# The last ten GpSimd weight-sum pieces moved from ahead of the expert groups into the first five down groups

## The reference

```
xn  = layernorm(x)
s   = attention(xn)      # q, k, v projections; phi = elu + 1;
                         # running sum over the sequence of phi(k) * v, times phi(q) * scale; then Wo
f   = ffn(xn)            # router to 8 experts, top 2, capacity 256 tokens each;
                         # every expert uses the same w1 (4096 x 1024, exact gelu) and w2 (1024 x 4096)
out = x + s * silu(f)
```

## Time and profile before

| what | value |
|---|---|
| median of 3 runs | 2046.07 us (2045.12 to 2046.35) |
| the profiled execution, its time | 2045.16 us |
| its span in the trace | 2043.1 us |
| mean granted TensorE clock | 0.991 |
| PE busy | 1983.1 us, 97% |
| DVE busy | 1378.4 us, 67% |
| ACT busy | 695.9 us, 34% |
| POOL busy | 513.2 us, 25% |

### The profile page before, as it was taken

How to read it: one execution, slowest core, us unless ns; L and a number is a source line. 1 busy time by engine, 2 the same in 40 slices (tenths; PEclk the granted TensorE clock), 3 DMA queues, 4 the chain that set the end, 5 groups by cost and what they waited for, 6 DMA issues and landing times.

```text
span 2043.1 us, 27171 instructions
## 1 busy us (share of the span) xinstructions
PE 1983.1 (97%) x9396; PEld 905.2 (44%) x9396; DVE 1378.4 (67%) x2090; ACT 695.9 (34%) x1094; POOL 513.2 (25%) x640
## 2 busy tenths in 40 slices
PE   8979999999899999999999999999999999999996
PEld 2335444554434444444444444444444444444442
DVE  3778888878867767767777787474554555456656
ACT  1422232222553453444345353343222212213322
POOL 0098888888711101101100010030000000000002
PEclk9989999999999999999999999999999999999998
DMA  9576766667999777876767878783333333334635
GB/s 356 203 243 224 241 231 211 222 220 217 306 373 269 211 250 217 230 255 213 252 233 238 284 240 288 250 220 111 108 98 103 103 103 98 104 119 139 200 108 130
DMA packets 185259, 419.93 MB, mean 206 GB/s; under 512 B 18816, under 2 KB 73664, under 8 KB 182720
## 3 DMA queue, kind: packets, MB, share of 16 engines
q1 hardware_dynamic: 141776, 287.93, 42.3%
q0 software_dynamic: 34912, 121.71, 20.3%
q10 hardware_dynamic: 8464, 8.92, 1.4%
HBM read 268.51 MB, written 166.77 MB: 213 GB/s over the span
## 4 chain that ended last, share of the span: by engine, by line
PE 67%; POOL 15%; DMA 9%; DVE 4%; issue 3%; ACT 1%; SPq 0%; ACTq 0%; DVEq 0%; POOLq 0%
PE pair L2005 34%; PE pair L1976 31%; DMA arena<-w_down 3%; DMA arena<-w_up 3%; PE pair L1768 2%; POOL arena L723 2%; POOL arena L735 2%; POOL arena L737 1%; POOL arena L746 1%; POOL arena L739 1%; POOL arena L748 1%; POOL arena L750 1%; POOL arena L740 1%; POOL arena L751 1%; POOL up_sums L729 1%
## 5 line engine op out<-in xcount | busy, mean ns | idle before, releaser
L2005 PE MATMUL pair<-arena 128*128 128x512 f16 x3360 | 731.4, 379 | 9.6 <-DVE arena L1564 2.5
L1976 PE MATMUL pair<-xnT,arena 128*128 128x512 f16 x2400 | 528.5, 381 | 8.4 <-ACT xnT L962 4.1
L2005 PEld LDWEIGHTS pair<-arena 128*128 128x128 f16 x3360 | 326.9, 98 | 410.8 <-issue 17.6
L1818 PE MATMUL pair<-arena 128*128 128x512 f16 x1728 | 388.2, 383 | 8.4 <-DVE xnT L454 7.6
L1589 DVE SCALAR_TENSOR_TENSOR arena<-pair,arena 128x1024 f32<-128x1024 f32 x234 | 286.1, 1223 | 157.6 <-PE pair L2005 157.2
L1976 PEld LDWEIGHTS pair<-xnT,arena 128*128 128x128 f16 x2400 | 234.9, 98 | 295.4 <-ACT xnT L962 6.9
L1031 ACT ACTIVATE arena<-arena 128x512 f16<-128x512 f32 x280 | 170.0, 625 | 565.1 <-PE pair L2005 503.6
L1818 PEld LDWEIGHTS pair<-arena 128*128 128x128 f16 x1728 | 169.4, 98 | 205.4 <-issue 16.4
L1976 PE MATMUL pair<-xnT 128*128 128x512 f16 x960 | 213.8, 379 | 0.0
L1564 DVE SCALAR_TENSOR_TENSOR arena<-arena 128x512 f16<-128x512 f32 x280 | 189.1, 684 | 20.2 <-ACT arena L1031 18.3
L772 POOL DMA_DIRECT2D s_dram<-arena x8 | 6.2, 778 | 596.6 <-DVE arena L1589 581.4
(11 more groups left out here) (203 smaller groups left out, 1822.9 us busy)
## 6 DMA issues: line engine op xcount, KB each, us to landing
down_dram<-arena SPq DMA_DIRECT2D x70, 512.0 KB, 4.5
arena<-down_dram SPq DMA_DIRECT2D x70, 512.0 KB, 3.3
up_dram<-arena SPq DMA_DIRECT2D x100, 256.0 KB, 5.0
arena<-up_dram SPq DMA_DIRECT2D x100, 256.0 KB, 2.6
arena<-w_up POOLq DMA_DIRECT2D x40, 512.0 KB, 5.3
up_sums<-arena POOLq DMA_DIRECT2D x40, 512.0 KB, 3.6
arena<-w_down POOLq DMA_DIRECT2D x40, 512.0 KB, 5.2
down_sums<-arena POOLq DMA_DIRECT2D x40, 512.0 KB, 3.8
```

Source lines behind the costliest of these rows:

```text
L1818: ins = mm(out_bank(n), xT[u][:, a, c, :], wkv[:, (n // 2) * CH + c, b, e], start=(c == 0 and i == 0), stop=(c == CH - 1 and i == 2), skip ...
L1976: ins = mm(out_to, w[:, a, c * P:(c + 1) * P], x_in_op[:, b, c, :], start=(first and i == 0), stop=(i == 11), skip_group_check=True)
L2005: ins = mm(bank[2 + t // 2][:, (t % 2) * BLOCK:(t % 2 + 1) * BLOCK], g_ops[:, A_NAMES.index(DOWN_A[j]), c, a, t * P:(t + 1) * P], down_rin ...
```

## The change

The first 70 pieces are made as before. The last ten have a place of their own, `late_sums`: four rows of 256 f32 of `xnT` (the low part of x block "12", which no product reads once the sums of x are made, and where from group 7 on `kvq` lies). They are made one after another, two to a down, for downs 0 to 4: a load at point p = 0 (piece one) and p = 4 (piece two), the four operations and the store at p = 2 and p = 6. Each load waits for the store of the piece before; the first waits for the sums of x. ACT waits for 70 instead of 80 stores before it writes into `sum_ring`'s bytes, and for all 80 before its first load into `kvq`.

```
+        LATE_UNITS = 10
+        late_sums = xnT_rows[:, 8:12, HOLE:2 * HOLE]
...
+            def unit_at(u):
+                return late_sums if u >= len(UNITS) - LATE_UNITS else sum_ring[u % 3]
+
             def load_unit(u):
...
-                pool.dma_start(sum_ring[u % 3], src[:, :, c * (BLOCK // 2):(c + 1) * (BLOCK // 2)]).then_inc(sum_loaded[u % 3], 16)
+                pool.dma_start(unit_at(u), src[:, :, c * (BLOCK // 2):(c + 1) * (BLOCK // 2)]).then_inc(sum_loaded[u % 3], 16)
...
-            load_unit(0)
-            load_unit(1)
-            for u in range(len(UNITS)):
+            def make_unit(u):
                 if UNITS[u][0] == "up":
                     up_unit(u)
                 else:
                     down_unit(u)
                 store_unit(u)
-                if u + 2 < len(UNITS):
+
+            in_time = len(UNITS) - LATE_UNITS
+            load_unit(0)
+            load_unit(1)
+            for u in range(in_time):
+                make_unit(u)
+                if u + 2 < in_time:
                     if u >= 1:
                         pool.wait_ge(sum_stored[(u - 1) % 3], 16 * ((u - 1) // 3 + 1))
                     load_unit(u + 2)
...
                     pool.dma_start(out_rows[i, p], x_rows[i, p]).then_inc(copied, 16)
+
+                    u = in_time + 2 * i + p // 4
+                    if u < len(UNITS):
+                        if p % 4 == 0:
+                            if u == in_time:
+                                pool.wait_ge(xsum_done, 32)
+                            else:
+                                pool.wait_ge(sum_stored[(u - 1) % 3], 16 * ((u - 1) // 3 + 1))
+                            load_unit(u)
+                        elif p % 4 == 2:
+                            make_unit(u)
...
-                    stored(act, len(UNITS))
+                    stored(act, len(UNITS) - LATE_UNITS)
...
                         act.wait_ge(meta_ready, 1)
+                        stored(act, len(UNITS))
```

More of the change, by code:

```diff
@@ L728, in store_unit @@
                 pool.wait_ge(sum_made, 4 * u + 4)
-                pool.dma_start(to[:, :, c * (BLOCK // 2):(c + 1) * (BLOCK // 2)], sum_ring[u % 3]).then_inc(sum_stored[u % 3], 16)
+                pool.dma_start(to[:, :, c * (BLOCK // 2):(c + 1) * (BLOCK // 2)], unit_at(u)).then_inc(sum_stored[u % 3], 16)
             def up_unit(u):
-                w11, w12, w22, w21 = (sum_ring[u % 3][:, b, :] for b in range(4))
+                w11, w12, w22, w21 = (unit_at(u)[:, b, :] for b in range(4))
                 pool.wait_ge(sum_loaded[u % 3], 16 * (u // 3 + 1))
```

## The result

The changed kernel takes 2041.84 us (median of 8 runs, 2038.3 to 2043.41) against 2045.97 (8 runs) of the kernel before: ratio 0.9976, 95% interval 0.9967 to 0.9986, a gain of 4.9 us with 2.9 to 6.8 possible (the two medians are 4.1 us apart). The forecast was 2036.1 us, a gain of 10. The time lies just within the range given (2033 to 2042), the gain is a little under half of what was forecast.

The account below looks back on a forecast made before the run. PE was taken as busy for 1983.1 of 2043.1 us, with late loads causing waits before down 0. A gain of 10.5 us less 0.5 in the downs gave 10.0: 2036.1 us against 2046.07, range 2033 to 2042.

Parts of the forecast that it names:

- The chain's 15% for POOL: Chain of waits over the whole span: its 300 us for POOL can't be the pieces' cost, exceeding PE's 60 us idle.
- The signs: Before down 0: PE's waits fall from 9.8 to about 4 us, down 0 starts near 607; later groups stay 72.5 us.
- the wait at 558: PE's wait for ACT's PSUM copy, behind splits with late loads: 3.1 us of it goes.
- the work around 528: PE's sums of x: the 0.5 us wait goes and the clock may hold, 0.5 + 1.5 = 2.0 us.
- the ring of ACT, DVE, SP and the two loads: From 565 us to down 0: loads take 7 and 5 us, so PE is free at 599.3, 10.5 us earlier.
- Rival 1: Before down 0, SP's own traffic keeps loads at 10.92 and 6.21 us: gain 4.9, 2041.2 us; chance 0.27.
- part 2: Ten pieces within downs 0 to 4: PE has no idle time there; cost 0.5 us, bounds nothing and 2.5 us.
- GpSimd's own queue: ... All three cost nothing: GpSimd's store waits, SP's loads of these sums and ACT's new wait for all 80 stores: no cost, hundreds of us cover.

## Why the prediction was half right

**Right: what bounds, and where.** No engine waits for the last pieces; their transfers make SP's loads late. The chain's 15% for POOL was not a cost: taking the ten pieces out of the run won 9.1 us, and with their transfers alone put back 7.1 us of that is gone again. This was shown. The signs came in part: PE's waits fell to 5.6 us (about 4 forecast), down 0 starts at 611.2 and 609.9 us (607), and each group after it takes 72.5 us as before.

**Right: the wait at 558 and the work around 528.** The wait of 3.33 us and its low clock are gone, and the 0.5 us before DVE's L1434 too. I put 2.0 us on the stretch of the sums of x, and it is 2.1 in both profiles. The clock part of it is luck in a single run, though (last section).

**Too large: the ring of ACT, DVE, SP and the two loads.** I put the gain from quad 0 to down 0 at 8.5 us (10.5 less the 2.0), measured are 7.0. The first load was given 7 us and took 8.2, the second 5 and took 6.5.

The mechanism is right and the sizes are off: from the first load's issue to PE it takes 42.2 us (561.21 to 603.40) instead of 44.6, and the two loads 14.7 instead of 17.1, so the ring shrank by just what its loads did, 2.4 us where I had 5.1. The first load is issued 6.5 us earlier against the sums of x, where I had 5.4, which made up for 1.1 of it.

The stretch from 575 to 615 us is full of SP's own traffic (share 1.00, 372 GB/s), part of which I had read as backlog. Rival 1 had named just that, and it is partly true: without the 4 MB of saves the second load leaves the chain and 1.9 us more are won. Its time, 2041.2 us, is the measured one almost to the digit, but by luck: it gave quads 0 to 2 a gain of 3.4 us (5.4 less the 2.0), they won 7.0, and the DRAIN took the difference.

**Right: part 2 costs PE little or nothing.** Down 0 to the last scatter is 1414.67 us in both first profiles and 1.0 us more in the changed kernel's second; I had given it 0.5 us. DVE's operations do stretch, as expected: L1587 from 611 to 990 us (min/median/max), where L1564 in the kernel before had 694 ns at most from 620 to 1250:

```profile
L1587 DVE SCALAR_TENSOR_TENSOR arena<-arena x72: 677/683/1206, 620.8 to 988.2; 128x512 f16<-128x512 f32 x72
```

It is GpSimd's operations that do it: the same line has 693 ns at most with the late transfers alone, and 1210 with the late operations alone. That decides nothing for ten pieces, since the adds, which read a product tile out of PSUM, keep their time (L1612 is 1212 to 1226 ns from 611 to 990 us, L1589 before 1215 to 1225). That the margin is small is true, but I looked for it at the adds: twenty pieces cost 4.9 us, by way of the splits in the quad behind.

**The step that failed** is the sentence "GpSimd's own queue: ... All three cost nothing". It asked who waits for what stands in the queue, and found nobody. The transfers moved to it have a cost that no instruction of the queue waits for: the DRAIN at its end is 3.3 us longer, and it is the last instruction of the kernel. That is the larger part of what is missing, and the two loads of the ring are the other (1.5 us):

| term | forecast | measured |
|---|---|---|
| sums of x | -2.0 | -2.1 |
| quads 0 to 2 | -8.5 | -7.0 |
| start of the sums of x | 0 | +0.2 |
| downs and all behind, to the last scatter | +0.5 | 0.0 and +1.0, mean +0.5 |
| tail | 0 | +3.3 |
| sum | -10.0 | -5.1 (runs: -4.9) |

Why late transfers lengthen the DRAIN is open. It isn't the number of all transfers on the queue (the kernel before has as many and 3131 ns), nor the operations, nor the stores alone. What GpSimd does in the DRAIN no view shows. That the time falls within the range is luck for that part: no term of the range stood for it.

## What to carry to other kernels

When work is moved off a crowded stretch, add up its transfers first: here they were worth three to four times the operations (7.1 against 2.0 us). The stretch that had a DMA share of 1.0 with the moved queue silent stayed full (371 GB/s before, 372 after); size the loads in such a stretch by what they take there, not by a calm one. Look at what an engine does at the end of its program, DRAIN included, before handing it late transfers (here it went from 3131 to 6397 ns), and issue them from another queue if it shows.

## What the runs showed that I had not expected

- GpSimd's last DRAIN takes 3131 ns to the digit in the profiles of seven different kernels, and 5.3 to 6.5 us with ten or more late transfers on its queue.
- After the same wait of 2.0 us at the same place (PE idle from 529.8 to 531.75 in the changed kernel), TensorE's granted clock stayed at 1.00 in six of the twelve profiles of the changed kernel and its variants in which the wait of 0.5 us ahead of it was gone, and fell to 0.50 in the others, which costs 1.7 us (27.2 or 28.9 us from the sums of x to quad 0). A longer idle time doesn't decide it either: in the kernel before without transfers PE waited 2.5 us there, and the clock stayed at 1.00. The changed kernel, then the one with loads ahead of saves, each over 2 us (the first still holds 0.75 us of the wait, the second begins 0.94 us behind it); PEclk is the third number from the end:

```profile
531.00:533.00 2.00, 1.25 (x6) 0.60 (x7) 1.86 (x7) 0.82 (x3) 0.00 (x0) 1.00 1.08 388
```

```profile
530.00:532.00 2.00, 2.00 (x6) 0.76 (x5) 2.00 (x5) 1.50 (x4) 0.00 (x0) 0.50 1.06 404
```

  In both, PE ran the same sequence at full pace up to the wait. So a term of 1.7 us for a clock that may hold should have been counted at half.
